# A three-tap convolution: bias with the middle tap on ScalarE, two multiply-adds on VectorE

## What is computed

```
h = bit_linear(layernorm(x), w1)          # 1024 -> 4096, activations rounded to 8 bits per token, weights to -1, 0, 1
h = depthwise_conv1d(h, conv_w, conv_b)   # 3 taps along the tokens: w0*h[t-1] + w1*h[t] + w2*h[t+1] + b, per channel
h = silu(h)
x = x + layernorm(bit_linear(h, w2))      # 4096 -> 1024, rounded again per token
```

## Time and profile before

| | |
|---|---|
| median of 3 runs | 1316.98 us (1315.31 to 1319.25) |
| profiled execution | 1316.7 us |
| its span on the slowest core (5) | 1315.2 us |
| spans of the cores | 1308.8 to 1315.2 us |
| granted TensorE clock, mean of core 5 | 0.950 |
| busy, core 5: TensorE, VectorE, ScalarE, GpSimd | 89%, 84%, 65%, 32% |

### The profile page before, as it was taken

One profiled execution on the slowest core, in us unless ns is written; L12 is line 12 of the kernel. 1 busy time (PEld: TensorE's weight loads), 2 busy tenths in 40 slices (PEclk: granted clock), 3 DMA queues, 4 the chain that ended last, 5 costly groups with the idle time before them and its releaser, 6 DMA issues.

```text
span 1315.2 us, 18619 instructions; the slowest of 8 cores (1308.8 to 1315.2 us)
## 1 busy us (share of the span) xinstructions
PE 1168.4 (89%) x6184; PEld 603.1 (46%) x6184; DVE 1106.9 (84%) x2302; ACT 855.1 (65%) x1131; POOL 419.2 (32%) x654
## 2 busy tenths in 40 slices
PE   0378898997666899999999999999999999999897
PEld 0256666774222444444444444444444444444442
DVE  0269889986999999999999999999999999888661
ACT  0798989998899666666666666666666666555001
POOL 1114222321774122244333224333322431212233
PEclk9998878888898899999999999999999999999898
DMA  9996689995661112111211111121211111010110
GB/s 206 319 331 218 186 256 292 311 310 185 207 198 44 46 39 75 49 48 50 80 49 65 49 49 49 54 76 48 65 49 49 49 51 47 33 33 33 63 67 33
DMA packets 40099, 146.51 MB, mean 111 GB/s; under 512 B 4804, under 2 KB 4804, under 8 KB 39748
## 3 DMA queue, kind: packets, MB, share of 16 engines
q1 hardware_dynamic: 39572, 142.69, 33.8%
q0 software_dynamic: 432, 2.62, 1.2%
HBM read 114.36 MB, written 33.55 MB: 112 GB/s over the span
## 4 chain that ended last, share of the span: by engine, by line
PE 69%; DVE 16%; ACT 5%; DMA 4%; SPq 2%; issue 2%; POOL 1%; POOLq 0%; DVEq 0%; ACTq 0%
PE pF L850 32%; PE pO L721 27%; DMA stg<-w1T 4%; PE pF L326 4%; SPq L72 2%; DVE h L760 2%; PE pO L372 2%; DVE xs L393 1%; DVE h L765 1%; DVE hsc L356 1%; PE pF L953 1%; DVE h L753 1%; PE pT L447 1%; DVE accP L780 1%; DVE ysb L361 1%
## 5 line engine op out<-in xcount | busy, mean ns | idle before, releaser
L850 PE MATMUL pF<-w2q,h 128*128 128x512 fp8e4 x2048 | 480.1, 380 | 1.8 <-DVE h L839 1.8
L721 PE MATMUL pO<-xqT,w1q 128*128 128x512 bf16 x1792 | 427.1, 382 | 5.6 <-ACT xqT L452 5.6
L850 PEld LDWEIGHTS pF<-w2q,h 128*128 128x128 bf16 x2048 | 200.6, 98 | 241.8 <-issue 4.6
L727 ACT ACTIVATE hp<-pO 128x512 bf16<-128x512 f32 x224 | 133.6, 596 | 218.8 <-PE pO L721 217.4
L721 PEld LDWEIGHTS pO<-xqT,w1q 128*128 128x128 fp8e4 x1792 | 175.2, 98 | 213.8 <-issue 10.8
L760 DVE SCALAR_TENSOR_TENSOR h<-hp,cwt,h 128x512 bf16<-128x512 bf16 x256 | 202.8, 792 | 0.7
L746 ACT ACTIVATE bt<-hp,cwt 128x512 bf16<-128x512 bf16 x256 | 183.9, 718 | 6.1
L772 ACT ACTIVATE h<-h 128x1024 bf16<-128x1024 bf16 x128 | 134.9, 1054 | 76.1 <-DVE h L765 75.7
L833 DVE TENSOR_TENSOR h<-h,bc 128x512 bf16<-128x512 bf16 x256 | 151.0, 590 | 0.0
L896 POOL TENSOR_SCALAR sm<-sm 128x1 f32<-128x1 f32 (+1 forms) x33 | 17.2, 522 | 376.6 <-DVE sm L883 376.6
L765 DVE TENSOR_TENSOR h<-h,bt 128x512 bf16<-128x512 bf16 x256 | 115.6, 452 | 14.7 <-ACT bt L746 1.3
(11 more groups left out here) (147 smaller groups left out, 1514.7 us busy)
## 6 DMA issues: line engine op xcount, KB each, us to landing
stg<-w1T SPq DMA_DIRECT2D x40, 512.0 KB, 15.3
xs<-x SPq DMA_DIRECT2D x32, 512.0 KB, 11.2
stg<-w2T SPq DMA_DIRECT2D x32, 512.0 KB, 9.1
x2c<-xs SPq DMA_DIRECT2D x32, 512.0 KB, 9.0
stgC<-w2T SPq DMA_DIRECT2D x32, 512.0 KB, 5.9
x2r<-x2c SPq DMA_DIRECT2D x31, 512.0 KB, 4.6
out<-yev SPq DMA_DIRECT2D x31, 512.0 KB, 3.0
x2q<-x2c SPq DMA_DIRECT2D x28, 512.0 KB, 3.3
```

What stands on the lines that cost most here:

```text
L721: p_w1[n] = P(lambda e, k=k: e.matmul(bankW1(n), w1q[:, HD * k + 128 * c:HD * k + 128 * (c + 1)], xT[:, :, k, :], start=(k == 0), stop=(k ...
L727: a_ev[n] = A(lambda e: e.activation(hp3[:, n % 8, 2:514], bankW1(n), AF.Identity), *((v_stt[n - 8], a_bt[n - 8], g_sv[n // 4 - 2]) if n > ...
L850: p_w2[m] = P(lambda e, c=c, jj=jj: e.matmul(pb[:, 512 * jj:512 * (jj + 1)], h43[:, ring(32 * f + c), 128 * g:128 * (g + 1)], w2q[:, D * c ...
```

## The change

The bias goes from VectorE's first instruction to ScalarE's `tap1`, as that activation's bias operand. `conv0` becomes a scalar_tensor_tensor that computes w0 * hp + bt, so it needs `bt` of its own tile where it needed only `evac`. `conv2` stays and is now the last of the three taps; `silu` waits for it. `conv1` is gone. `tap1` now waits for `conv0` of three tiles before (it frees `bt`) instead of `conv1`.

```diff
         def tap1(n):
             c = n % 32
             a_bt[n] = A(lambda e: e.activation(bt[n % 3][:, :], hp3[:, n % 8, 1:513], AF.Identity,
+                                               bias=cbt[:, c:c + 1],
                                                scale=cwt[:, 3 * c + 1:3 * c + 2]),
-                        v_cv[n - 3] if n >= 3 else None, a_ev[n], g_re[n // 4])
+                        v_ts[n - 3] if n >= 3 else None, a_ev[n], g_re[n // 4], v_idb, d_small[2])

         def conv0(n):
             c, H_ = n % 32, h43[:, ring(n), :]
             old = n - NH4
-            v_ts[n] = V(lambda e: e.tensor_scalar(H_, hp3[:, n % 8, 0:512], cwt[:, 3 * c:3 * c + 1],
-                                                  cbt[:, c:c + 1], OP.mult, OP.add),
+            v_ts[n] = V(lambda e: e.scalar_tensor_tensor(
+                H_, hp3[:, n % 8, 0:512], cwt[:, 3 * c:3 * c + 1], bt[n % 3][:, :], OP.mult, OP.add),
                         p_w2[32 * (old // 32) + 24 + (old % 32) // 4] if old >= 0 else None,
-                        g_re[n // 4], a_ev[n])
+                        g_re[n // 4], a_bt[n])

         def conv2(n):
             c, H_ = n % 32, h43[:, ring(n), :]
-            v_stt[n] = V(lambda e: e.scalar_tensor_tensor(
+            v_stt[n] = v_cv[n] = V(lambda e: e.scalar_tensor_tensor(
                 H_, hp3[:, n % 8, 2:514], cwt[:, 3 * c + 2:3 * c + 3], H_, OP.mult, OP.add), v_ts[n])
-
-        def conv1(n):
-            H_ = h43[:, ring(n), :]
-            v_cv[n] = V(lambda e: e.tensor_tensor(H_, H_, bt[n % 3][:, :], OP.add),
-                        v_stt[n], a_bt[n])
...
-            if cv is not None:
-                conv1(cv)
```

## The result

The changed kernel takes 1322.18 us (median of 6 runs) against 1317.14 of the kernel before, run beside it: a ratio of 1.0036 (95% interval 1.0024 to 1.0049), which is 3 to 6.5 us slower. One of the six runs (1473.53) fell into a second, slower state of the chip, in which four cores show a granted clock of about 0.86, and the ratio goes by the other five. The profiled execution took 1322.15 us, with a span of 1320.6 us on its slowest core (3); the cores lie between 1312.9 and 1320.6.

A forecast was written before the change was run, and what follows sets the result against it. TensorE bounds the steady stage; VectorE and ScalarE run the fill in lockstep. Fill +3.5, boundaries -0.5, w2 start +0.3 and end +0.5 give +3.8 on 1316.7: 1320.5 us, range 1311.5 to 1325.5.

The forecast's parts named there:

- VectorE's own work, nothing saved in the even step: VectorE's convolution: an even step takes 2.52 us before and after; an odd step gets 0.11 us shorter.
- The new wait in the fill, +1.3 a period for 2.7 periods, +3.5: Fill: conv0 waits for its tap, `kw` gets in, silu waits; +3.5 us, bounds -2.2 and +4.9.
- three silu waits of 0.65: Fill: three of four pairs a period delay silu by 0.65 us, 1.95 in place of 0.67 waited before.
- The bias costs nothing on the tap: ScalarE's tap: the added bias operand costs 0, as the bias rides along with a scale already there.
- the upper bound of 0.13: ScalarE's tap: at most 0.13 us more each from the bias, 3.4 us over 26 steps.
- ScalarE's own period of 24.2: Fill: a period of 8 steps of ScalarE's own work without waits, 24.2 us against 24.91 before.
- Steady stage, -0.1 at each boundary: Five scale boundaries: VectorE's lateness vanishes behind a stretched instruction, -0.1 us each, -0.5 in all.
- the slower rival: Scale boundaries: VectorE's lateness is not swallowed, five times +0.65 in place of -0.1, 1324 us; chance 0.2.
- The start of w2, +0.3: Start of w2: the first quant_rnd stands behind a conv0 that is 0.33 us longer, +0.3 us.
- The end, +0.5: End: conv0 starts 0.72 us later and has less done when `yev` gets in; +0.5 us, upper bound +0.7.
- the -2.1: End: the favourable bound, -2.1 us if conv2 gets through before `yev` and silu starts by 1218.
- Rule and row: VectorE: the skill's rule made 256 fewer instructions a gain; the trace rows gave the even step none.

The follow-up runs named there:

- the two experiments that take away one of them: Changed kernel with conv0 reading zeros, not bt, so not waiting for the tap: 1309.85 us; changed kernel with GpSimd's `kw` on 16 of 1024 columns: 1310.08 us.
- e1 to e5: Bias alone moved, 1312.27 us; change without bias, 1319.75; change with conv0 reading zeros, 1309.85; `kw` on 16 columns in changed kernel, 1310.08, and in kernel before, 1310.94.
- the small `kw`: GpSimd's w2 rounding `kw` on 16 of 1024 columns, in the changed kernel (1310.08 us) and in the kernel before (1310.94 us), one run each.
- e2_no_bias: Changed kernel without the tap's bias operand, so the bias is left out of the computation: 1319.75 us, ratio 1.0024 to the kernel before.
- the wait taken away: Changed kernel with conv0 reading a tile of zeros in place of bt, so it waits for evac alone: 1309.85 us, ratio 0.9947 to the kernel before.
- e1_bias_only: Kernel before with only the bias moved to the tap on ScalarE, VectorE keeping its three instructions: 1312.27 us, ratio 0.9974.
- e6_tap_early: Changed kernel with the tap directly behind its own evac in ScalarE's list: 1321.86 us, ratio 1.0055 to the kernel before.

## Why the prediction was right, and where it was off

The forecast of 1320.5 us was 1.7 below the median. The side, slower, had 0.38, less than the 0.44 of no change. That the number came so close is in part luck: the sum forecast +3.8 and the stages on the cores compared give +3.4, but only because the fill lost 0.8 more than forecast and the steady stage gained 1.1 more. The first part, which the sum leaves out, adds 2.1 in the profiled execution. (The upper end of the range, worked out by its own terms, is 1325.7 and not 1325.5.)

- *VectorE's own work, nothing saved in the even step.* Right. An even step that nothing disturbs, from its conv0 to the next, before (core 5) and after (core 3):

```profile
369.09 0.41 DVE L753 TENSOR_SCALAR h<-hp,cwt,cbt 128x512 bf16<-128x512 bf16 x1
...
371.62 1.22 DVE L753 TENSOR_SCALAR h<-hp,cwt,cbt 128x512 bf16<-128x512 bf16 x1
```

```profile
419.78 0.75 DVE L755 SCALAR_TENSOR_TENSOR h<-hp,cwt,bt 128x512 bf16<-128x512 bf16 x1
...
422.31 0.74 DVE L755 SCALAR_TENSOR_TENSOR h<-hp,cwt,bt 128x512 bf16<-128x512 bf16 x1
```

  It takes 2.53 us in both; the sum had 2.52.
- *The new wait in the fill, +1.3 a period for 2.7 periods, +3.5.* The mechanism was right in its place, its parts and their order, and it needs both parts, as the two experiments that take away one of them show. The term was mis-sized: a period lost 2.0 and not 1.3, and the fill 4.3 and not 3.5. All three full periods counted, where the forecast had 2.7: against the first evac the fourth tap comes 1.0 sooner than before (15.8 us in place of 16.8) and the 28th 4.8 later (94.6 in place of 89.8). The 1.0 gained in the first steps had no term; the kernels e1 to e5 have 0.8 to 1.2 of it too. The forecast had three silu waits of 0.65; they were 0.29, 0.72 and 0.31, where the 0.72 stands behind a conv2 (at 381.38) stretched to 1.60 while conv0 went free. The step that failed is that silu's wait was the only one counted: L435 waits 0.47 us for VectorE, since L428 to L432 stand behind an accN of 1.52 us, and ScalarE's own period became longer (next item).
- *The bias costs nothing on the tap.* Wrong in the instruction, right in this kernel's time. It costs 0.09 us each (0.718 to 0.810), inside the upper bound of 0.13. The Trainium skill (ScalarE: Activation LUTs, What ACT_TABLE_LOAD costs) states about 93 ns for each pointer operand of an ACTIVATE; 0.718 to 0.810 agrees. As a price on a full ScalarE it is 0.75 a period, as the small `kw` shows. Behind the stretched conv0 it makes no difference: leaving it out gives 0.05 a period, since the waits grow by as much as the taps shrink (in e2_no_bias the silu waits of a period are 0.47, 1.06 and 0.50 where they are 0.29, 0.72 and 0.31).
- *The bias taken from VectorE's tensor_scalar* had no term at all. It is worth 0.061 us an instruction, and shows only where that instruction is kept; the change throws it away with the tensor_scalar.
- *ScalarE's own period of 24.2.* It is 23.89. The list of waits shows one of 0.67 a period before, and the small `kw` another 0.35 that no row names.
- *Steady stage, -0.1 at each boundary.* Right in sign, too small: -1.0 over four boundaries. The changed kernel with the wait taken away has 456.6 where the change has 456.7, so the wait costs nothing there; what shortens the boundaries wasn't isolated. VectorE's lateness does vanish, as predicted: TensorE's waits are 2.7 us in five, not the 6 of the slower rival. From the sixth join to the seventh the distance grows from 112.7 to 113.8 with the wait and stays at 112.6 without it, but from the seventh join to the last tap it is 0.9 shorter, so the stage is no longer for it.
- *The start of w2, +0.3.* TensorE's wait at the first w2 matmul (L850, now L847) grew from 0.5 to 0.8 us. The size is the forecast one; whether by its cause isn't shown, since the bias-only kernel, with a shorter conv0, waits 1.2 there.
- *The end, +0.5.* Right: 7.6 to 8.1, and 7.3 with the wait taken away. Changed kernel, core 3, answering to the earlier trace rows:

```profile
1220.11 0.81 ACT L746 ACTIVATE bt<-hp,cbt,cwt 128x512 bf16<-128x512 bf16 x1
...
1220.95 0.75 DVE L755 SCALAR_TENSOR_TENSOR h<-hp,cwt,bt 128x512 bf16<-128x512 bf16 x1 [0.48 <-ACT bt L746]
...
1222.43 0.74 DVE L762 SCALAR_TENSOR_TENSOR h<-hp,cwt,h 128x512 bf16<-128x512 bf16 x1
...
1223.70 1.05 ACT L769 ACTIVATE h<-h 128x1024 bf16<-128x1024 bf16 x1
1223.88 2.42 POOL L908 TENSOR_TENSOR yev<-yev,x2r 128x1024 f32<-128x1024 f32 x1 [0.66 <-ACT yev L904]
1224.14 2.32 DVE L836 TENSOR_SCALAR h<-h 128x512 bf16<-128x512 bf16 x1
```

  conv2 does get through ahead of `yev`, and silu starts 3.6 us after the tap began (it was 5.0); that was the place of the -2.1. It gains nothing, since `yev` (2.42 us) now runs beside a rounding (L836), stretched to 2.32 in place of 0.28, that stands in VectorE's list ahead of the join. The size was right and the path to it wasn't the one told.
- *Rule and row.* By the Trainium skill (VectorE: DVE Perf Modes, Rules for kernel authors) fewer VectorE instructions were to be a gain. The count fell by 256 and the time rose by 0.36%, while the kernel that keeps all three instructions and shortens one is 0.26 to 0.46% faster than before (3.0 us, 0.23%, by its stages).

**The version to keep** is the bias alone moved to ScalarE: 1312.27 and 1310.45 us in two sessions, against 1316.13 and 1317.34 before and 1322.18 for the change as made.

## What to carry to other kernels

Count a merged instruction by its start-to-start times, and then ask what it newly waits for: here VectorE was relieved of 33 us of recorded busy time, an even step of it got no shorter, and the kernel lost 5 us, 3.6 of them shown in its stages, to one wait and what got in during it. A gap that opens on an engine is not free time if another engine, shut out until then, uses it to start something long; look at what was queueing for the gap. And split a change in two before judging it: moving the bias, made alone, is a gain here that the whole change doesn't have.

## What the runs showed of the hardware

- A 128x512 activation with scale and bias from memory takes 0.810 us (after), with the scale alone 0.718 (before, e2_no_bias).
- A 128x512 bf16 tensor_scalar takes 0.408 us with two scalar operands (multiply and add; before), 0.347 with one (multiply; e1_bias_only), in the median.
- On ScalarE an instruction that reads what the one ahead wrote starts 0.66 us after it (365.22 to 365.88 in e6_tap_early), one that doesn't 0.48 (367.87 to 368.35, after), behind an evac of 0.57 us.
- conv0 that starts 0.57 us into a `kw` of 1.19 loses 0.42 (1.17 less 0.75), while `kw` loses nothing. The Trainium skill (SBUF — State Buffer, SBUF: two separate sides) has whoever starts first keep the shared ports for its whole instruction. That the late one bears the loss agrees; it loses 0.2 less than the 0.62 that `kw` had still to run by its record. Not every pair goes by who starts first: in the kernel before, a `kw` that starts at 363.60 is the one that is stretched (1.73 us), while the accP that starts 0.07 later keeps its 0.68.
- An even step of VectorE in the fill takes 2.53 us from conv0 to conv0 with three instructions for the convolution (before) and with two (after): tensor_scalar and tensor_tensor together cost what one scalar_tensor_tensor does.
